# Two heads' P cast in one ScalarE operation in the first cross attention, and both small attentions' steps laid out anew

## What is computed

```python
# layer 0, cross attention: H = 32, D = 16, keys and values from ctx
q = apply_axial_rope((x @ Wq).reshape(b, n, H, D), pos_map)
k, v = jnp.split(ctx @ Wkv, 2, axis=-1)          # k gets rope as well
logits = jnp.einsum('bqhd,bkhd->bhqk', q, k) * scale
w = jax.nn.softmax(logits, axis=-1)
attn = jnp.einsum('bhqk,bkhd->bqhd', w, v).reshape(b, n, H * D)
return attn @ Wout + bout
# layer 1, self attention: H = 16, D = 32, 4 groups, causal
scores = jnp.einsum('bqgsd,bkgd->bgsqk', q, k) * scale
attn = jax.nn.softmax(jnp.where(causal, -jnp.inf, scores), axis=-1)
return jnp.einsum('bgsqk,bkgd->bqgsd', attn, v).reshape(b, n, 512) @ Wo + bo
```

## Time and profile before

| | us |
|---|---|
| median of 3 launches | 3378.43 (3375.62 to 3384.37) |
| the profiled execution's own time | 3379.68 |
| its span, first to last instruction | 3377.7 |
| PE busy | 2857.4 (85%) |
| DVE busy | 2074.5 (61%) |
| ACT busy | 1771.8 (52%) |
| POOL busy | 1409.7 (42%) |

### The profile page before, as it was taken

The page is one execution under the profiler, slowest core; times in us unless marked ns, Lnnn a source line. Parts: engine busy times, 40 slices in busy tenths (PEclk is TensorE's granted clock), DMA queues, the critical chain, the costliest instruction groups (busy, mean ns, idle before and its releaser), DMA issues. The chain is left out here.

```text
span 3377.7 us, 64410 instructions
## 1 busy us (share of the span) xinstructions
PE 2857.4 (85%) x24866; PEld 2022.3 (60%) x24866; DVE 2074.5 (61%) x4462; ACT 1771.8 (52%) x3857; POOL 1409.7 (42%) x1537
## 2 busy tenths in 40 slices
PE   3999999947888884999999888878999999975787
PEld 1666666624666663777777666666666677642333
DVE  4667767756777765455555456655555555565886
ACT  3555555546888884233332266654444444454775
POOL 1444444425887881444444434451111112213553
PEclk9999999978999986999999999999999999997899
DMA  4000000010000004000000001002010110031000
GB/s 163 1 1 1 1 1 1 1 66 1 2 2 2 2 2 158 1 7 7 1 1 1 26 30 39 14 1 69 14 32 32 38 38 1 1 100 50 13 13 26
DMA packets 41189, 81.49 MB, mean 24 GB/s; under 512 B 5683, under 2 KB 9781, under 8 KB 40758
## 3 DMA queue, kind: packets, MB, share of 16 engines
q1 hardware_dynamic: 40886, 77.38, 6.8%
HBM read 73.18 MB, written 4.19 MB: 23 GB/s over the span
## 5 line engine op out<-in xcount | busy, mean ns | idle before, releaser
L1072 POOL TENSOR_TENSOR c_pT<-c_prob,c_pT 128x512 f16<-128x512 f32 x256 | 293.3, 1159 | 102.8 <-ACT c_pT L1029 102.2
L1925 POOL TENSOR_TENSOR c_prob<-c_prob,c_inv 128x512 f32<-128x512 f32 x128 | 133.5, 1043 | 310.5 <-DVE c_inv L2149 310.5
L1072 POOL TENSOR_TENSOR a_pT<-a_prob,a_pT 128x384 f16<-128x384 f32 x128 | 120.7, 945 | 189.9 <-ACT a_pT L1029 189.5
L733 DVE SCALAR_TENSOR_TENSOR a_pT<-psT,a_kvh_t,a_pT 128x256 f16<-128x256 f32 (+1 forms) x256 | 94.6, 410 | 169.6 <-ACT a_pT L642 169.6
L1263 ACT ACTIVATE c_prob<-psT 128x512 f32<-128x512 f32 x256 | 156.1, 610 | 69.4 <-PE psT L1194 55.4
L1344 DVE TENSOR_REDUCE c_peak<-psS 128x2 f32<-128x512 f32 x256 | 169.6, 683 | 20.5 <-PE psS L1175 17.2
L444 POOL TENSOR_TENSOR a_q_rot<-a_q_cos,a_q_sin 128x512 f32<-128x512 f32 x64 | 81.1, 1267 | 193.1 <-DVE a_q_sin L752 193.1
L1029 ACT CAST c_pT<-c_prob 128x512 f16<-128x512 f32 x256 | 159.9, 625 | 0.0
L2073 ACT CAST c_pT<-psT 128x512 f16<-128x512 f32 x128 | 74.8, 584 | 140.5 <-PE psT L1937 140.5
L2065 ACT ACTIVATE c_prob<-psS,c_negmax 128x256 f32<-128x256 f32 x256 | 119.2, 474 | 44.5 <-DVE c_negmax L2142 40.8
L463 POOL TENSOR_TENSOR a_prob<-a_prob,a_inv 128x128 f32<-128x128 f32 x128 | 52.4, 409 | 214.3 <-DVE a_inv L726 214.3
(11 more groups left out here) (630 smaller groups left out, 11387.7 us busy)
## 6 DMA issues: line engine op xcount, KB each, us to landing
c_feed<-in_L_ffn_w1T SPq DMA_DIRECT2D x16, 512.0 KB, 3.8
c_feed<-in_L_ffn_w2T SPq DMA_DIRECT2D x16, 512.0 KB, 3.7
f_stage<-in_f_up_gateT SPq DMA_DIRECT2D x16, 352.0 KB, 7.0
x_all<-in_x SPq DMA_DIRECT2D x1, 4096.0 KB, 14.3
a_stage<-in_L_attn_WqT SPq DMA_DIRECT2D x8, 512.0 KB, 7.5
a_stage<-in_L_attn_WoutT SPq DMA_DIRECT2D x8, 512.0 KB, 10.1
a_feed<-in_L_xattn_Wq SPq DMA_DIRECT2D x8, 512.0 KB, 3.7
c_feed<-in_L_xattn_Wo SPq DMA_DIRECT2D x8, 512.0 KB, 3.8
```

What stands on the lines that cost most here:

```text
L733: last = dve.scalar_tensor_tensor(pT[1][:, r, m, m * P:N], T[:, m * N + m * P:(m + 1) * N], kvh_t[:, b % 2, m, H + h:H + h + 1], pT[0][:, ...
L1072: pool.tensor_tensor(pT[1][:, c % NPH, :], prob[:, c % NPX, :], pT[0][:, c % NPH, :], ALU.subtract)\
L1925: pool.tensor_tensor(prob[:, h % NPB, :, :], prob[:, h % NPB, :, :], inv[:, h % NPB, :].rearrange("p (n a) -> p n a", a=1).broadcast_to([P ...
```

## The change

For the first cross attention only, PAIR is 2: `round_p` is called at each even step and casts heads t-2 and t-1 at once (1024 columns), and `prob` has four buffers instead of three. `low_p` stays one operation for each head. In both attentions all k stacks are now moved by DVE and all q stacks by ACT; `fill_slots` multiplies by a constant column held in a tile (a TENSOR_TENSOR) instead of by an immediate (a TENSOR_SCALAR); POOL fills that tile once; PV becomes 7, and the slots of most pieces move.

```diff
-    NPX, NPH = 3, 6
+    PAIR = 2 if from_ctx else 1
+    NPX, NPH = 4 if from_ctx else 3, 6
...
             if kind == "sk":
-                return "act" if n % 2 else "dve"
+                return "act" if sk_uses[n][0] == "q" else "dve"
...
-            return s.p_hi_act, c + 1
+            return s.p_hi_act, c // PAIR + 1
 
         def round_p(eng, copy, c):
-            eng.wait_ge(s.e_done, c + 1)
+            eng.wait_ge(s.e_done, c + PAIR)
             if c >= NPH:
-                eng.wait_ge(s.pv_done, c - NPH + 1)
-            copy(pT[0][:, c % NPH, :], prob[:, c % NPX, :]).then_inc(p_high(c)[0], 1)
+                eng.wait_ge(s.pv_done, c - NPH + PAIR)
+            copy(pT[0][:, c % NPH:c % NPH + PAIR, :], prob[:, c % NPX:c % NPX + PAIR, :]).then_inc(p_high(c)[0], 1)
...
+                pool.memset(shift[:, :], -1.0 / SHIFT).then_inc(s.zeroed, 1)
...
-                    if 0 <= t - 1 < B * H:
-                        round_p(act, act.copy, t - 1)
+                    if 0 <= t - PAIR < B * H and t % PAIR == 0:
+                        round_p(act, act.copy, t - PAIR)
...
-                    dve.tensor_scalar(q_stack[:, b % 2, :, heads, 3, 0], peak[:, heads, 0:NT].rearrange("p h n -> p n h"),
-                                      -1.0 / SHIFT, None, ALU.mult).then_inc(s.slot_done, 1)
+                    dve.tensor_tensor(q_stack[:, b % 2, :, heads, 3, 0], peak[:, heads, 0:NT].rearrange("p h n -> p n h"),
+                                      shift[:, 0:1].rearrange("p (n h) -> p n h", n=1).broadcast_to([P, NT, GH]),
+                                      ALU.mult).then_inc(s.slot_done, 1)
...
-                    {"k0": 0, "k1": 1, "x0": 2, "x1": 4, "q0": 5, "q1": 7, "o0": 8, "o1": 9, "y0": 17, "y1": 20,
-                     "v0": 24, "v1": 26, "sk": [6, 8, 10, 11, 12, 13, 14, 15], "S": 18, "peak": 27, "PV": 5})
+                    {"k0": 1, "k1": 1, "x0": 2, "x1": 2, "q0": 6, "q1": 7, "o0": 8, "o1": 9, "y0": 15,
+                     "y1": 20, "v0": 24, "v1": 31, "sk": [9, 9, 11, 12, 12, 12, 15, 17], "S": 21,
+                     "peak": 29, "PV": 7})
...
-                    {"x0": 0, "x1": 0, "kv0": 1, "kv1": 2, "q0": 3, "q1": 4, "o0": 5, "o1": 6, "y0": 11, "y1": 12,
-                     "sk": [4, 5, 7, 7, 8, 8], "S": 10, "peak": 14, "PV": 5}, G.a1, fed)
+                    {"x0": 0, "x1": 0, "kv0": 2, "kv1": 5, "q0": 4, "q1": 8, "o0": 9, "o1": 11, "y0": 13,
+                     "y1": 15, "sk": [5, 6, 7, 9, 9, 9], "S": 10, "peak": 14, "PV": 7}, G.a1, fed)
```

More of the change, by code:

```diff
@@ L944, in small_attention @@
         peak = sc.sb("peak", [P, H, PIECES], F32)
+        shift = sc.sb("shift", [P, 1], F32)
         inv = sc.sb("inv", [P, NT, GH], F32)
@@ L1218, in pv @@
                     last.then_inc(s.pv_done, 1)
-                pe.wait_ge(s.zeroed, 7 if HB > 1 else 5)
+                pe.wait_ge(s.zeroed, 8 if HB > 1 else 6)
                 for t in range(FIRST, LAST):
@@ L1283, in value @@
                     return act.copy(v_ones[0][:, b % NV, n, :, 0:D], src.rearrange("p (h d) -> p h d", d=D))
-                act.wait_ge(s.zeroed, 7 if HB > 1 else 5)
+                act.wait_ge(s.zeroed, 8 if HB > 1 else 6)
                 for t in range(FIRST, LAST):
@@ L1288, in _ @@
                         rows = slice(n * P, (n + 1) * P)
-                        turned_stack = kind == "sk" and n % 2
+                        turned_stack = kind == "sk" and frees_bank(kind, n) == "act"
                         if kind in ("x", "o", "v", "kv", "peak") or turned_stack or (kind == "q" and not from_ctx):
@@ L1434, in _ @@
                     dve.memset(halves[0:GD, :, :, 1, :], 0.0).then_inc(s.zeroed, 1)
-                dve.wait_ge(s.zeroed, 7 if HB > 1 else 5)
+                dve.wait_ge(s.zeroed, 8 if HB > 1 else 6)
                 for t in range(FIRST, LAST):
@@ L1441, in _ @@
                             rotate_parts(b, kind, n)
-                        elif kind == "sk" and n % 2 == 0:
+                        elif kind == "sk" and frees_bank(kind, n) == "dve":
                             dve.wait_ge(s.bank_ready, use[kind, b, n] + 1)
```

## The result

The changed kernel takes 3371.7 us in the median, the kernel before 3381.7 beside it: ratio 0.9969, 95% interval 0.9961 to 0.9977. That is 10 us faster, where 40 were forecast; it lies inside the stated range (3304 to 3378), but the gain is a quarter of the forecast one, and that it lies there is luck: it is the sum of a stage that gained more than forecast and one that lost. The profiled execution took 3371.6 us, its span is 3369.6 us, 8.1 less than before.

A forecast was written before the change was run, and what follows sets the result against it. No engine is full in the first cross attention, where PE, ACT and POOL hold each other; PE bounds the second self attention. From 3379.7 us, -17.5 and -22 give 3340.2, or 3339 as the runs' median; range 3304 to 3378.

The forecast's parts named there:

- the chain of 2.87 a pair: First cross attention: cast, subtraction, exponential and hops sum to 2.87 us a pair, against 2.43 before; last batch 45.7 us.
- the wait for `o_rows`: Second self attention: PE's wait, 2.55 us a batch, goes because o0 moves two whole steps behind the PV: -2.5.
- PE is always two turned heads ahead in such a chain: First cross attention: PE's lead over the pair's chain covers bursts; heads 12 to 32 take 29.0 us, 2.0 less.
- the 1.7 a batch given back for slips: First cross attention: allowance of 1.7 us a batch for half-clock stretches and short hops, leaving -3.0 a batch.
- the second half's sum (28.7 and 0.3): First cross attention, heads 12 to 32: ten pairs of 2.87 us, plus 0.3 for y0, give 29.0.
- y1 was taken to fit in 3.7 us: First cross attention: PE's 3.6 us of work around y1 fits before head 21's exponential, due after 3.7 us.
- The first half: First cross attention, heads 0 to 12: walking the queues gives 26.8 us a batch, 2.7 less than 29.5.
- the pair's chain decides: First cross attention: bursts come on top of the chain, 7 us more a batch; kernel slower at 3410 us; chance 0.12.
- -22 forecast: Second self attention: shorter waits and less half clock, less new q-stack waits, give -3.5 us a batch, -22 in all.
- The half clock: Second self attention: the slow-clock stretch after the wait for o costs 1.5 us a batch; 1.0 of it goes.
- L1350's median of 0.22: Nearest row for `fill_slots` as TENSOR_TENSOR, worst 0.87 us; taken as speaking mostly against its waiting like the old form.
- The rival had 0.13: `fill_slots`: the new form waits like the old, so 0.6 us a batch stays and the kernel takes 3343; chance 0.13.

The follow-up runs named there:

- the pair alone: Kernel before with only the cast of two heads and four `prob` buffers in the first cross attention, old slots, `fill_slots` as TENSOR_TENSOR: 3414.4 us, ratio 1.0092.
- the first run of this call: POOL's `add_parts` and `stack_lo` set ahead of the step's subtraction, against the pair alone: 3395.4 us, ratio 1.0032.
- the second self attention alone: Changed kernel with the first cross attention put back (one cast a head, three buffers, old slots and stack rule): 3355.2 us, ratio 0.9916.
- All but the pair, three buffers: Changed kernel with one cast a head and three `prob` buffers, all else kept: 3340.1 us, ratio 0.9870.

## Why the pair costs: experiments

With the pair alone the last batch took 46.0 us. That is the forecast of 45.7 from the chain of 2.87 a pair. But a full batch grew by 4.1 us, to 64.6. The chain was the first to be tried: six buffers for `prob` (and four for `pT`, to make room), old slots.

```diff
-    NPX, NPH = 4 if from_ctx else 3, 6
+    NPX, NPH = (6, 4) if from_ctx else (3, 6)
```

> As the pair alone (old slots), but six buffers for prob and four for pT, so that the subtraction of a pair no longer stands between its cast and the next pair's. Theory 1 (the loss is that chain): undisturbed exponentials return to 1.22 us a head, POOL's speed, the last batch to 43 to 44 us, the full ones to 60 or less; the kernel 15 to 40 us faster than the pair alone. Theory 2 (the loss lies in the slots or in the cast itself): no more than 5 us faster than the pair alone.

It bore out neither theory. The last batch fell to 41.5 us, under that of the kernel before: where nothing but heads runs, the chain was the limit and more buffers lift it. The full batches stayed at 62.7 to 65.7 (the pair alone: 63.6 to 64.8), and the whole is some 12 us faster than the pair alone. Cut at head 12, the full batches say more (means of six): heads 12 to 32 took 33.9 us with the pair alone and 31.8 with six buffers, heads 0 to 12, where k, q and the stacks are prepared, 30.7 and 32.2; before they took 32.1 and 28.4. So in the first part of a batch something else costs about 4 us. That `pT` has four buffers there is not seen to matter: ACT waits for a PV ahead of its casts for 2.4 us in the whole run.

What it is shows in POOL's and ACT's timelines of the pair alone (start, us; idle before and its releaser in brackets), batch 2, heads 2 to 6. POOL:

```profile
930.20 1.15 POOL L1075 TENSOR_TENSOR c_pT<-c_prob,c_pT 128x512 f16<-128x512 f32 x1 [0.58 <-ACT c_pT L1031]
931.32 1.26 POOL L1061 TENSOR_TENSOR c_part<-c_part 128x512 f32<-128x512 f32 x1
932.54 1.15 POOL L1075 TENSOR_TENSOR c_pT<-c_prob,c_pT 128x512 f16<-128x512 f32 x1
933.66 1.26 POOL L1061 TENSOR_TENSOR c_part<-c_part 128x512 f32<-128x512 f32 x1
936.17 1.16 POOL L1075 TENSOR_TENSOR c_pT<-c_prob,c_pT 128x512 f16<-128x512 f32 x1 [1.26 <-ACT c_pT L1031]
```
and ACT:
```profile
929.09 1.04 ACT L1031 CAST c_pT<-c_prob 128x1024 f16<-128x1024 f32 x1
930.02 0.59 ACT L1303 CAST c_xT<-psP 128x512 f16<-128x512 f32 x1
930.50 0.61 ACT L1266 ACTIVATE c_prob<-psT 128x512 f32<-128x512 f32 x1
932.62 0.63 ACT L1280 ACTIVATE c_k_stack<-c_part 128x512 f16<-128x512 f32 x1 [1.50 <-POOL c_part L1061]
```

POOL stood 0.58 us because the pair's cast ended late; behind the subtraction in its queue stood k's sum (L1061, `add_parts`), which needs no cast; ACT, done with its exponential, then waited 1.50 us for that sum, and with it the next exponentials and the next cast (at 935.05), for which POOL waited 1.26. The same engines wait for each other by turns. If that is the loss, k's and q's operations set ahead of the subtraction in POOL's step must help with the pair, and not without it:

```diff
-                    if 0 <= t - 2 < B * H:
-                        low_p(t - 2)
                     if from_ctx:
                         for kind, b, n in pieces_at(t - 2):
...
                                 stack_lo(b, kind, n)
+                    if 0 <= t - 2 < B * H:
+                        low_p(t - 2)
```

> The pair alone (3414), with POOL's add_parts and stack_lo ahead of the step's subtraction instead of behind it. Theory A (with the pair, the subtraction at the head of POOL's queue waits for a cast that comes a step later, and the pieces behind it come late to ACT and PE): 10 to 25 us faster than the pair alone, full batches of 61 to 63 us, less waiting of ACT for c_part. Theory B (the loss is the longer cast and the bursts on PE; POOL's order is of no account): within 5 us of 3414.

> Control for the first run of this call: the kernel before (one cast a head) with POOL's add_parts and stack_lo ahead of the step's subtraction. Theory A (the order matters through the pair's late cast): within 6 us of the kernel before. If the order is worth as much here as with the pair, 10 us or more, theory A says nothing about the pair.

And the cast itself can be early: behind the second exponential of its own pair, not behind the first of the next.

```diff
-                    if 0 <= t - PAIR < B * H and t % PAIR == 0:
-                        round_p(act, act.copy, t - PAIR)
+                    if PAIR == 2:
+                        if 0 <= t - 1 < B * H and t % 2:
+                            round_p(act, act.copy, t - 1)
...
```

> The pair alone (3414), with the cast right behind the second exponential of its pair (odd step) instead of behind the first of the next pair. Theory A (the lateness of the cast is the loss, in POOL's queue): POOL's wait for the cast falls from 90 us to 70 or less, full batches of 61 to 63, 10 to 25 us faster than the pair alone; the last batch, where the chain has one exponential less after the subtraction but ACT waits for the exponential's end, 43 to 46. Theory B (bursts on PE): full batches stay above 64, within 5 us of 3414.

Both were then made to the changed kernel with its new slots; the early cast waits for the PV of one head more, so PV is 6 there:

> The changed kernel (3371.7, late cast of the pair, new slots) with POOL's add_parts and stack_lo ahead of the step's subtraction. If the pieces stuck in POOL's queue behind the late cast are the loss here too: 10 to 25 us faster, full batches of the first cross attention 60 to 61.5 instead of 63.2. If in the new slots it is the waits for DVE (k's moves, row maxima): within 5 us.

> The changed kernel (3371.7) with the cast of the pair right behind its own second exponential, and PV 6 instead of 7 in the first cross attention, since the cast then waits for the PV of one head more. If the late cast is the loss as with the old slots (there the early cast took back 31 us): 3340 plus or minus 5, the last batch of the first cross attention about 40 us instead of 47.7. If the new slots have already used the room that the early cast gives: 3355 or more.

| | median, us | ratio (95%) | first | last batch | heads 0 to 12 | heads 12 to 32 |
|---|---|---|---|---|---|---|
| the kernel before | 3381.7 | 1 | 463.4 | 43.2 | 28.4 | 32.1 |
| the pair alone | 3414.4 | 1.0092 (1.0075 to 1.0109) | 493.3 | 46.0 | 30.7 | 33.9 |
| with six buffers | 3400.9 | 1.0059 (1.0042 to 1.0075) | 481.1 | 41.5 | 32.2 | 31.8 |
| with POOL's pieces first | 3395.4 | 1.0032 (1.0021 to 1.0044) | 478.0 | 46.0 | 29.1 | 33.5 |
| with the early cast | 3383.8 | 1.0003 (0.9994 to 1.0013) | 463.8 | 39.7 | 28.7 | 32.7 |
| kernel before, POOL's pieces first | 3387.3 | 1.0016 (1.0007 to 1.0026) | 470.1 | 43.3 | 28.9 | 32.7 |
| the whole change | 3371.7 | 0.9969 (0.9961 to 0.9977) | 483.2 | 47.7 | 26.4 | 36.7 |
| with POOL's pieces first | 3360.3 | 0.9945 (0.9924 to 0.9966) | 472.3 | 47.7 | 25.9 | 35.6 |
| with the early cast, PV 6 | 3339.3 | 0.9874 (0.9858 to 0.9891) | 453.8 | 41.1 | 25.8 | 33.9 |
| no pair, four buffers | 3329.7 | 0.9848 (0.9831 to 0.9866) | 443.8 | 40.5 | 25.9 | 32.4 |

The last two columns are means of batches 1 to 6, from exponential to exponential.

POOL's order is worth 0.60% with the pair, and without it costs 0.16%: the control goes the other way. With the pair alone the gain is in heads 0 to 12, 30.7 to 29.1, where six buffers gained nothing. So the pair costs in two ways: through the chain, which six buffers lift, and through what stands behind the late cast in POOL's queue, which the order lifts. In the new slots the order is worth 0.24%, with intervals that overlap, and a full batch is 61.6 us for 63.2: less than with the old slots. In the trace the wait that was to go is gone. Where the pair alone has, among ACT's waits over six batches,

```profile
ACT c_prob L1266 <- PE psT L1197: 59.3, 41, 3.9
...
ACT c_k_stack L1280 <- POOL c_part L1061: 9.0, 6, 1.5
```
the run with POOL's pieces first has no such line, and the first one is shorter (ACT's wait for the subtraction grew, from 15.0 to 19.7 us):
```profile
ACT c_prob L1266 <- PE psT L1197: 53.0, 36, 3.0
```

The early cast takes back 0.89% of 0.92, and in the new slots 0.95%. Its last batch, 39.7 us, is the shortest of all: exponentials come in twos, and the cast stands right behind them (ACT, start and duration):

```profile
1246.02 1.04 ACT L1031 CAST c_pT<-c_prob 128x1024 f16<-128x1024 f32 x1
1246.97 1.25 ACT L1266 ACTIVATE c_prob<-psT 128x512 f32<-128x512 f32 x2
1248.25 1.04 ACT L1031 CAST c_pT<-c_prob 128x1024 f16<-128x1024 f32 x1
1249.79 1.12 ACT L1266 ACTIVATE c_prob<-psT 128x512 f32<-128x512 f32 x2 [0.49 <-POOL c_pT L1075]
```

So most of the price is not the cast of 1024 columns but its place: one exponential and one step too late for POOL. Cast early, the pair in the old slots comes back to the kernel before, which has three buffers. It never beat one cast a head at the same four buffers: 3339 against 3330 on the same chip (ratios 0.9874 and 0.9848 with intervals that overlap), 453.8 us against 443.8 in the stage. There 29 of the pair's 39 us are its place; the other 10 are left with the early cast, or come of its PV 6, which was not run by itself.

**What the new slots add to it.** In the changed kernel heads 0 to 12 of batch 3 took 26.7 us (26.8 forecast) and heads 12 to 32 took 36.4 (29.0 forecast; 31.0 before). Of the 7.7 us over ten undisturbed pairs (28.7), 3.7 are between heads 12 and 13, 2.1 between 15 and 16 (y0 in slot 15), 1.8 between 20 and 22 (y1 in slot 20). ACT from the exponentials of heads 11 and 12 (one row) to head 16's:

```profile
1009.51 1.07 ACT L1266 ACTIVATE c_prob<-psT 128x512 f32<-128x512 f32 x2
1010.47 1.05 ACT L1031 CAST c_pT<-c_prob 128x1024 f16<-128x1024 f32 x1
1011.71 1.01 ACT L1252 COPY c_qS<-psP 128x1024 f16<-128x1024 f16 x1 [0.19 <-PE psP L1136]
1014.25 1.01 ACT L1252 COPY c_qS<-psP 128x1024 f16<-128x1024 f16 x1 [1.52 <-PE psP L1136]
1015.16 0.60 ACT L1266 ACTIVATE c_prob<-psT 128x512 f32<-128x512 f32 x1
...
1018.18 0.61 ACT L1266 ACTIVATE c_prob<-psT 128x512 f32<-128x512 f32 x1
1018.69 1.01 ACT L1252 COPY c_qS<-psP 128x1024 f16<-128x1024 f16 x1
1021.72 0.60 ACT L1266 ACTIVATE c_prob<-psT 128x512 f32<-128x512 f32 x1 [2.02 <-PE psT L1197]
```
DVE and PE behind the second copy:
```profile
1011.03 1.25 DVE L1354 TENSOR_TENSOR c_q_stack<-c_peak,c_shift 128x16 f16<-128x16 f32 x1
1012.15 0.67 DVE L1256 COPY c_kS<-psP 64x1024 f16<-64x1024 f16 x1
1012.84 0.69 DVE L1257 COPY c_kS<-psP 64x1024 f16<-64x1024 f16 x1
```
```profile
1013.59 0.62 PE L1136 MATMUL psP<-ident_h,c_q_stack 128*128 128x128 f16 x8 [1.92 <-DVE c_kS L1257]
```

Three stacks stand in slot 12. The third needs the bank of the first, a k stack, which DVE moves; DVE was held 1.25 us by `fill_slots`; PE stood 1.92 us; the second of ACT's two copies stood ahead of head 13's exponential, 5.2 us after head 12's. Then y0 (slot 15) found PE without a lead, and head 16's scores came 2.02 us late. This stall is there without the pair too: in the run with four buffers the exponential of head 13 comes 4.4 to 5.2 us after head 12's in batches 1 to 6. But there the undisturbed heads after it come 1.0 us apart, and with the pair 1.4: the pair has no speed to catch up with. That the two work together so is read from the traces; the runs show the sum: heads 12 to 32 take 32.4 us in that run and 36.7 in the changed kernel, heads 0 to 12 take 25.9 and 26.4.

## The second self attention: experiments

The forecast put the largest term on the wait for `o_rows`, 2.55 us a batch. Its edit alone, on the kernel before:

```diff
-                    {"x0": 0, "x1": 0, "kv0": 1, "kv1": 2, "q0": 3, "q1": 4, "o0": 5, "o1": 6, "y0": 11, "y1": 12,
+                    {"x0": 0, "x1": 0, "kv0": 1, "kv1": 2, "q0": 3, "q1": 4, "o0": 7, "o1": 8, "y0": 11, "y1": 12,
```

> The kernel before with one edit in the second self attention: o0 and o1 in slots 7 and 8 instead of 5 and 6. If the wait for o_rows is the main part of what the new slots gain there and takes the half clock with it: no wait of L1150 for a_o_rows, clock 0.98 or more, six batches of 250 us become 230 to 235, the kernel 13 to 20 us faster than before. If the gain is in many small waits, or o now queues behind the stacks of slots 7 and 8: at most 8 us faster.

Nothing was gained: 3386.4 us, ratio 1.0007 (0.9998 to 1.0017), the stage 308.9 us, the clock still 0.95. PE's longest waits between 1993.08 and 2242.95 (its batches 1 to 6 but for the last 7 us) were then

```profile
PE psP L1143 <- DVE a_q_stack L1351: 19.8, 18, 2.0
PE psP L1150 <- DVE a_qS L1249: 11.9, 10, 4.1
```

The wait for `a_o_rows` (15.3) is gone as expected, and 11.7 us came back as waiting for `fill_slots` (8.1 before), 11.9 as o waiting for a bank that DVE's move of q frees. The wait for o had covered both. Is it then the rule, that q is ACT's? The two parts, run apart: new slots and PV 7 with the old rule (against the run of the second self attention alone), and the old slots with the new rule (against the kernel before; only the rule is shown). The first cross attention is as before in both.

```diff
-                return ("act" if n % 2 else "dve") if from_ctx else ("act" if sk_uses[n][0] == "q" else "dve")
+                return "act" if n % 2 else "dve"
```

> The second self attention with its new slots and PV 7 but the old rule for the stacks (even ones DVE, odd ones ACT); the first cross attention as before. With both it was 3355 (25 us faster than before). If the slots are the gain: 3352 to 3360. If it needs q's moves off DVE (where they waited behind fill_slots and held o back): 3365 or more.

```diff
-                return "act" if n % 2 else "dve"
+                return ("act" if n % 2 else "dve") if from_ctx else ("act" if sk_uses[n][0] == "q" else "dve")
...
```

> The kernel before with the new rule for the stacks in the second self attention and nothing else. If the rule is the gain: 3365 or less. If the slots are: within 5 us of before, 3377 to 3387.

| | median, us | ratio (95%) | second |
|---|---|---|---|
| o later | 3386.4 | 1.0007 (0.9998 to 1.0017) | 308.9 |
| new slots, old rule | 3359.5 | 0.9932 (0.9915 to 0.9948) | 282.0 |
| old slots, new rule | 3388.7 | 1.0023 (1.0012 to 1.0035) | 314.0 |
| both | 3355.2 | 0.9916 (0.9899 to 0.9933) | 273.5 |

The slots as a whole, with PV 7, are the gain: 0.68% of 0.84. The rule alone costs 0.23%, a little more than its expectation allowed; with the new slots it takes 8.5 us off the stage (282.0 to 273.5), though the two ratios' intervals overlap. What PE waits for in batches 1 to 6 of the changed kernel:

```profile
PE psP L1136 <- DVE a_k_stack L1401: 5.7, 6, 1.7
PE psP L1136 <- DVE a_q_stack L1394: 4.6, 6, 0.8
PE psS L1178 <- DVE a_peak L1347: 4.6, 7, 1.1
PE psS L1178 <- ACT a_qS L1252: 2.8, 6, 0.5
PE psP L1136 <- ACT a_qS L1252: 2.6, 6, 1.2
```

No wait is over 1.7 us, and the clock is 1.00 in this stretch. Before, waits of 2.55 us stood ahead of half-clock stretches. Which of the moved slots (kv, q, o, y and five of the six stacks) or PV 7 carries it stays open: only o was moved alone, and only to slots 7 and 8.

## `fill_slots`: an experiment

All but the pair, three buffers, with the immediate back:

```diff
-                    dve.tensor_tensor(q_stack[:, b % 2, :, heads, 3, 0], peak[:, heads, 0:NT].rearrange("p h n -> p n h"),
-                                      shift[:, 0:1].rearrange("p (n h) -> p n h", n=1).broadcast_to([P, NT, GH]),
-                                      ALU.mult).then_inc(s.slot_done, 1)
+                    dve.tensor_scalar(q_stack[:, b % 2, :, heads, 3, 0], peak[:, heads, 0:NT].rearrange("p h n -> p n h"),
+                                      -1.0 / SHIFT, None, ALU.mult).then_inc(s.slot_done, 1)
```

> All but the pair (3340) with fill_slots as the TENSOR_SCALAR of before. If both forms wait for GpSimd's operation alike: within 4 us of 3340, DVE's operation of 16 columns again near 1 us in the median where it was 0.6 as TENSOR_TENSOR. If the new form spares the wait: 5 us or more slower.

3340.4 us, ratio 0.9876 (0.9859 to 0.9892); with TENSOR_TENSOR it was 3340.1, 0.9870: no difference. First that run's instructions, then those of its twin with the TENSOR_TENSOR (ns min/median/max):

```profile
L1354 DVE TENSOR_SCALAR c_q_stack<-c_peak x32: 203/442/1061, 796.7 to 1240.3; 128x16 f16<-128x16 f32 x32
```
```profile
L1354 DVE TENSOR_TENSOR c_q_stack<-c_peak,c_shift x32: 230/466/1093, 797.2 to 1244.5; 128x16 f16<-128x16 f32 x32
```

The two forms wait alike. The fall of the median from 1025 ns to 624 in the changed kernel comes of where the operation falls beside POOL's, not of its form; my expectation of a return to 1 us was wrong in the same way. The traces show it one by one. Of the 32 operations of the changed kernel in the first cross attention, 27 start while a TENSOR_TENSOR of POOL runs and has over 0.2 us to go, and each of them ends 0.08 to 0.09 us after that one; before, it is 27 of 32, and 0.06 to 0.07 us. The other five take 0.23 us (before 0.20 to 0.21). The longest, 1.25 us from 1011.03, has this POOL operation beside it (start and duration):

```profile
1010.94 1.26 POOL L1093 TENSOR_TENSOR ln_r<-x_all,c_bias 128x512 f32<-128x512 f32 x1
```

## Why the prediction failed, step by step

- **The chain of the pair** held: cast 1.04 for 1.06, links as read; the last batch with the pair alone 46.0 us for 45.7. In the changed kernel it was 47.7; a stall at y1 came on top.
- **"PE is always two turned heads ahead in such a chain"** is the step that failed, and with it heads 12 to 32: 36.7 us in the mean of six batches for 29.0, 7.7 a batch or 46 over six; the 1.7 a batch given back for slips covers 10 of them. The whole miss in this stage is 35. The step treated a period that is longer than PE's need as a cushion in which bursts vanish. It is one only as long as nothing upstream stalls, and a chain with no slack never makes up what a stall costs. It failed without the new slots too: the pair alone took 33.9 us there, 1.8 more than before, and not less. In batch 3 of the changed kernel the terms are these. The three stacks of slot 12 fall behind head 12, and the second half's sum (28.7 and 0.3) has no term for them: they cost 3.7 us, 1.25 us of `fill_slots` in them. y0 behind them was taken to cost 0.3 and cost 2.1. y1 was taken to fit in 3.7 us with 0.1 to spare and cost 1.8.
- **The first half** came out near its sum, 26.4 us in the mean (26.7 in batch 3) for 26.8, but the gain was taken from a wrong base. That base of 29.5 is the mean batch less the second half of batch 3, which is one of the shortest; the mean halves before are 28.4 and 32.1 (60.5 together). So the forecast was a gain of 1.6 there, not of 2.7, and it was 2.0. The rival "the pair's chain decides", with 0.12, named the right part and the right sign, 16 x 0.44 = 7 us a batch; the pair's measured price, 41 us in the new slots at equal buffers, is most of its 56. But its mechanism was only half: six buffers lift the chain and leave most of the loss. The other half is order in POOL's queue behind a late cast, for which the prediction has no term.
- **The fourth buffer** was a part of the change that I did not cost apart from the pair: 8.5 us in the stage without the pair.
- **The new slots of the first cross attention**: never summed by themselves. They gain 11 us.
- **The second self attention**: -22 forecast, -30.8 in the trace, and 25 us by the median, 28 by the ratio, when it was changed alone. The wait for o went, as forecast; but as a cause it was wrong, since alone it gains nothing. The half clock was taken at 1.0 a batch and gave 1.4 (8.5 us of PE in six).
- **`fill_slots`**: I took 0.25 to 0.9 us and mostly the low end, on L1350's median of 0.22. It measured 0.23 to 1.25, with a median of 0.62. The reading of L1350 was wrong: its median says where those operations fell, mostly behind a POOL operation with under 0.22 us to go, and all that started earlier beside one end 0.02 us after it, as `fill_slots` does with 0.09. The Trainium skill (SBUF — State Buffer, "SBUF: two separate sides") says that a DVE operation with two SBUF inputs is blocked by a GpSimd operation that reads SBUF and started first. This trace agrees: 1.25 us for 16 columns that otherwise take 0.23, while POOL works. The rival had 0.13. Its condition came true, the new form waits like the old; its 4 us did not come, since PE's wait for this operation in the second self attention fell from 8.1 us to 0.6 with the new slots. But the 1.25 stood in the stall of slot 12.
- **No other stage moved**, as said: 2.0 us between the attentions and -1.5 behind them.

The version that beats both is the changed kernel with one cast a head and four buffers: 3329.7 us, 1.5% under the kernel before.

## What to carry to other kernels

Joining two operations saves only what the engine's own overlap does not already hide (here 0.05 us a pair, not the 0.18 that the durations, 1.04 and twice 0.61, suggest), and it delays the first of them by a step: ask who waits for the result and what stands behind that wait in the waiting engine's queue. If two must be joined, issue the joined one right behind the last thing it needs. And a wait that covers two others is worth nothing by itself; take a change apart with the buffers apart from the operation, since the part that pays may be the one that came along.

## What the runs showed of the hardware that was not expected

A DVE operation of 16 columns that took 0.23 us alone took up to 1.25 beside POOL with two SBUF inputs (changed kernel), and 0.20 and up to 1.21 with an immediate operand (kernel before). Its end follows that of POOL's TENSOR_TENSOR by 0.09 and 0.06 us. ACT's cast of 128x1024 from f32 to f16 took 1.04 us where two of 128x512 took 0.61 each, yet ACT's queue moved on 0.95 us after its start (1246.02 to 1246.97) against about 0.50 after each single one: in occupancy the two are nearly the same.
